# Another table of turns for a two-layer decoder: readers of norms, the router's choice and the tail's selection stand one or two turns later

## The reference

```
x = norm(x + splat_attention(x))          # 16 heads of 16, 256 keys, scores over 16 gaussians
x = norm(x + cross_attention(x, ctx))     # 16 heads of 16, 120 keys
x = norm(x + gate * expert[argmax](x))    # router over 8 experts, one 256x256 expert a token
x = norm(x + causal_attention(x))         # 16 heads of 16
y = norm_gain(x)                          # then two blocks, each:
y = y + block(y, y or ctx)                #   attention, 16 heads of 32, + li1, norm, li2 (1024), gelu, li3
x = norm(x + y)                           #   first block: 256 keys, kept only after the diagonal; second: ctx
x = norm(x + sum of 4 of 16 experts(x))   # sigmoid gates, top 4, hidden 64 an expert
```

## Time and profile before

| | |
|---|---|
| median of 3 runs | 3736.54 us (3733.85 to 3744.52) |
| the profiled execution | 3735.17 us |
| its span, first to last instruction | 3733.0 us |
| TensorE busy, matmuls | 3110.0 us, 83% |
| VectorE, ScalarE, GpSimd busy | 2682.5, 2104.6, 972.8 us |
| mean granted TensorE clock | 0.922 of full |
| idle of TensorE ahead of the transposes of `z` (L727) | 98.8 us on `z`, in 39 waits |
| on the key ring's DMA (L710) | 79.5 us, in 36 waits |

### The profile page before, as it was taken

The page is one execution under the profiler, slowest core; times in us unless marked ns, Lnnn a source line. Parts: engine busy times, 40 slices in busy tenths (PEclk is TensorE's granted clock), DMA queues, the critical chain, the costliest instruction groups (busy, mean ns, idle before and its releaser), DMA issues. The chain is left out here.

```text
span 3733.0 us, 89796 instructions
## 1 busy us (share of the span) xinstructions
PE 3110.0 (83%) x34864; PEld 2446.6 (66%) x34864; DVE 2682.5 (72%) x6391; ACT 2104.6 (56%) x4254; POOL 972.8 (26%) x1788
## 2 busy tenths in 40 slices
PE   1978888888788888988988888898988897988886
PEld 1767666767676767766766666676766676766664
DVE  5768676767676767767777667686776777868765
ACT  4746665556556554664565555646665556466642
POOL 0312341122233321231233222212342122124310
PEclk9999899989899989989999989998998999989987
DMA  6211211112212121121121111212121112112110
GB/s 199 71 55 58 74 57 61 44 44 60 64 50 77 50 63 43 49 67 53 48 74 58 54 54 38 70 45 72 59 69 60 38 42 70 48 60 71 60 37 6
DMA packets 362009, 221.50 MB, mean 59 GB/s; under 512 B 102497, under 2 KB 333299, under 8 KB 361587
## 3 DMA queue, kind: packets, MB, share of 16 engines
q1 hardware_dynamic: 361586, 215.76, 19.1%
HBM read 122.23 MB, written 93.32 MB: 58 GB/s over the span
## 5 line engine op out<-in xcount | busy, mean ns | idle before, releaser
L1150 ACT ACTIVATE p<-bank,p_log 128x512 f32<-128x512 f32 (+2 forms) x1280 | 748.4, 585 | 1104.1 <-PE bank L839 989.4
L1711 POOL TENSOR_TENSOR prob<-p,prob 120x256 f16<-120x256 f32 (+2 forms) x512 | 450.4, 880 | 1644.7 <-ACT prob L1151 1644.3
L1151 ACT ACTIVATE prob<-bank,p_log 128x512 f16<-128x512 f32 (+2 forms) x1280 | 749.6, 586 | 0.0
L1416 DVE TENSOR_REDUCE negm<-bank 128x2 f16<-128x512 f32 (+1 forms) x1024 | 511.3, 541 | 91.1 <-PE bank L803 87.7
L1339 DVE TENSOR_TENSOR prob<-p,prob 128x512 f16<-128x512 f32 (+2 forms) x768 | 487.8, 644 | 91.6 <-ACT prob L1151 87.5
L710 PE MATMUL bank<-w_exp,ident_h 128*128 128x512 f16 x1280 | 419.8, 412 | 95.6 <-DMA k_ring<-k_heads 79.5
L818 PE MATMUL bank<-q_ring,k_ring 80*128 80x256 f16 (+4 forms) x2048 | 443.7, 283 | 41.1 <-ACT raw L1097 14.6
L839 PE MATMUL bank<-ident_h,negm 128*128 128x256 f16 (+2 forms) x2560 | 441.4, 260 | 0.0
L1720 POOL TENSOR_SCALAR_AFFINE_SELECT probm<-prob 128x128 f16<-128x128 f16 x1024 | 327.2, 358 | 299.0 <-DVE prob L1339 299.0
L803 PEld LDWEIGHTS bank<-k_ring,q_ring 80*128 80x128 f16 (+1 forms) x2560 | 236.6, 104 | 234.3 <-issue 52.6
L803 PE MATMUL bank<-k_ring,q_ring 80*128 80x256 f16 (+4 forms) x2560 | 361.7, 259 | 33.9 <-DVE negm L1416 22.6
(11 more groups left out here) (293 smaller groups left out, 6261.9 us busy)
## 6 DMA issues: line engine op xcount, KB each, us to landing
q_ring<-q_heads SPq DMA_DIRECT2D x768, 40.0 KB, 2.1
q_heads<-q_made SPq DMA_DIRECT2D x96, 256.0 KB, 2.3
k_heads<-k_made SPq DMA_DIRECT2D x96, 256.0 KB, 2.3
q_ring<-q_heads SPq DMA_DIRECT2D x512, 48.0 KB, 2.1
k_ring<-k_heads SPq DMA_DIRECT2D x512, 40.0 KB, 2.2
q_heads<-q_made SPq DMA_DIRECT2D x144, 128.0 KB, 1.8
k_heads<-k_made SPq DMA_DIRECT2D x144, 128.0 KB, 1.8
k_ring<-k_heads SPq DMA_DIRECT2D x256, 48.0 KB, 2.2
```

The source lines that it names most:

```text
L1150: act(p32[0:n, g % PBUF32, 0:cols], ps[0:n, 0:cols], ACT.Exp, bias=p_log[0:n, :], scale=a.scale)
L1151: act(prob[0:n, 0, g % PBUF, 0:cols], ps[0:n, 0:cols], ACT.Exp, bias=p_log[0:n, :], scale=a.scale).then_inc(a_done, one(a_done))
L1416: v.tensor_reduce(negm[:, h * NT:(h + 1) * NT], scores[:, :].rearrange("p (t n) -> p t n", t=NT)[:, :, 0:ATTNS[k].keys], AX.X, ALU.max, ne ...
L1711: g.tensor_tensor(prob[0:n, 1, m % PBUF, 0:cols], p32[0:n, m % PBUF32, 0:cols], prob[0:n, 0, m % PBUF, 0:cols], ALU.subtract).then_inc(pp_ ...
```

## The change

The table gets other numbers. Nothing else is changed: no instruction is added or taken out, and each engine keeps the order of its stages but for those that now pass parts of the attention or a stage of another chain. Three stages of `LATE_SOON` come earlier by one.

```diff
@@ -152,20 +152,20 @@
 EARLY = {
     0: (),
     1: (("oT", 9), ("out", 12), ("out2", 14)),
-    2: (("oT", 9), ("out", 11), ("out2", 12), ("xT_e", 15), ("router", 17), ("best", 21), ("experts", 22), ("experts2", 26), ("experts3", 30)),
+    2: (("oT", 9), ("out", 11), ("out2", 12), ("xT_e", 16), ("router", 18), ("best", 22), ("experts", 24), ("experts2", 27), ("experts3", 30)),
     3: (("oT", 9), ("out", 13), ("norm2", 14), ("norm4", 19)),
     4: (("oT", 9), ("out", 11), ("out2", 12), ("ctx", 16), ("ctx2", 17), ("xoT", 18), ("h0", 22), ("h1", 23), ("h2", 26), ("norm3", 28), ("norm4", 30)),
-    TAIL: (("oT", 9), ("out", 11), ("out2", 12), ("xoT", 16), ("h0", 18), ("h1", 21), ("h2", 25), ("h3", 26), ("xT", 29), ("sel", 31)),
+    TAIL: (("oT", 9), ("out", 11), ("out2", 12), ("xoT", 17), ("h0", 19), ("h1", 22), ("h2", 25), ("h3", 26), ("xT", 31), ("sel", 33)),
 }
 LATE = {
     0: (("xT", 2), ("q_raw", 4), ("q", 7), ("k_raw", 10), ("k", 15), ("v", 18)),
     1: (("xT", 2), ("q", 9), ("k", 10), ("v", 13)),
     2: (("xT", 1), ("q", 10), ("k", 13), ("v", 18)),
     3: (("xT", 4), ("q", 9), ("k", 14), ("v", 17)),
-    4: (("xT", 1), ("q", 10), ("k", 14), ("v", 16)),
-    TAIL: (("gates", 2), ("r0", 4), ("r1", 8), ("r2", 10), ("r3", 11)),
+    4: (("xT", 3), ("q", 10), ("k", 14), ("v", 16)),
+    TAIL: (("gates", 4), ("r0", 6), ("r1", 9), ("r2", 11), ("r3", 12)),
 }
-LATE_SOON = {1: (("xT", 18), ("q", 21), ("k", 23), ("v", 28)), 3: (("xT", 22), ("q", 24), ("k", 25), ("v", 28))}
+LATE_SOON = {1: (("xT", 18), ("q", 20), ("k", 22), ("v", 27)), 3: (("xT", 22), ("q", 24), ("k", 25), ("v", 28))}
 VECTOR_ONLY = ("out2", "experts3", "norm4", "h3", "r3", "ctx2")
 ENGINES = "tensor", "scalar", "vector", "gpsimd"
```

## The result

The changed kernel takes 3826.26 us (median of 4 runs, 3815.76 to 3827.52) beside 3740.41 us for the kernel before in the same job: ratio 1.0219, 95% interval [1.0202, 1.0236], 82 us slower by the ratio (the medians lie 86 us apart). The prediction was 3751, range 3705 to 3782. Its direction held, its size did not: the time lies outside the range.

A forecast was written before the change was run, and what follows sets the result against it. TensorE, busy 83% of the span, was taken as the bound, waiting only where a turn precedes its data. Terms -2 + 0 + 3 - 13 + 5 + 17 + 5 + 0 = +15 us on 3735.17 gave 3750, as median 3751; range 3705 to 3782.

The forecast's parts named there:

- The sum leaves this as it is: TensorE's clock: about 580 us at the lower level stay, since old waits shrink and new ones of 1 to 2 us come.
- The tail's block at 0, bounds -24 and +12: (TAIL, xT), sel, gates, r0 later: shorter waits offset by the later choice and split of `inT`; 0 us, bounds -24 and +12.
- Rival 1: Tail and (4, xT): the choice of four and the masks are never late; -15 us, 3721 us; chance 0.2.
- r1, r2, r3 at +3, bounds 0 and +8: Tail's r1 to r3 one turn later: some 0.5 us less cover for `hidT` between r1 and r2; +3 us.
- (2, xT_e), router, best at -13, bounds -17 and -8: Stages of k = 2, later past R: 14 waits on `x` shorten, -14, router +1, best 0; -13 us.
- experts, experts2 at +5, bounds 0 and +8: Stages of k = 2, later: half of W less ahead of (2, xT), which already waits on `x`; +5 us.
- (TAIL, xoT), h0 at +17 and h1 at +5: Tail, one turn later: ScalarE's features behind exponentials delay h0, +17 us; less cover ahead of h2, +5 us.
- (4, xT) at -2: Turn 1 to 3, past W: shorter waits on `z`, against losses where masked attention makes W wait; -2 us, bounds -8 and +6.
- LATE_SOON at 0: q, k, v one turn earlier: gain or loss taken up by the key ring's DMA wait; 0 us, bounds -5 and +5.
- the signs named: TensorE's waits: `x` to about 18 us, `z` about 75, `tailT` gone, `raw` and `oT` up 15 to 20, new `inT` wait.
- Rival 4: Tail: h0 waits 2 us in all 16 tails (+32), the choice of four loses 12; +42 us, 3778 us; chance 0.15.

## Why the prediction was wrong, step by step

The steps that failed are the price of 0 for the tail's late block, which cost 43 to 49 us, the -13 for the router's stages, which cost 11, and the +3 for r1, which cost 12 to 18 of the block's; and the sum had no term for TensorE's busy time.

- **"The sum leaves this as it is"** (the clock) failed: the time at the lower level rose by 36 us in the traces and by 59 as means, worth at most 18 or 30 us. These are the same microseconds as those of the stages below, not a cause beside them. Half of the span's 80.8 us is busy time, and what part of it the clock does not explain stays open.
- **The tail's block at 0, bounds -24 and +12**: 43 to 49 us. The order of events was right (ScalarE's four exponentials, then the choice, then the split of `inT`), and the new wait at q_raw was named. The sizes were off. The choice was put to end 0.5 us later than now and the split at 648.05, where TensorE needs it at 648.54; no working is given for the 0.5. Counted from the transposes' start, the choice ends at 8.01 us where I had 6.7, and was at 6.18 before. Of these 1.83 us, 1.34 are the later start of sel's exponential (4.25 us behind the transposes, 2.91 before) and 0.49 the first step of the choice, which takes 0.67 us beside GpSimd's pass in place of 0.18. R and E between `z` and sel are at the lower level, R 1.25 us (646.72 to 647.97) where it takes 0.65 at full clock (656.99 to 657.64, the fence with r1 on 8); but they were so before too (1.21 us from 643.35), so a sum from the old trace should have had it. And in the phase shown what follows the wait runs slower as well. Rival 1 decided "from the point where q_raw waits under 0.5 us"; it waits 1.92.
- **r1, r2, r3 at +3, bounds 0 and +8**: 17.6 us alone, 12 beside sel on 32. I counted what lies between r1 and r2 and not what lies ahead of r1: that turn 9 has oT, that the lower k goes first, and that r1's 6.3 us had been the cover of `o_tok`. The sentence on it is missing, not mis-sized.
- **(2, xT_e), router, best at -13, bounds -17 and -8**: +11. The gain at `x` came (10.6 us in the list); a stage with the same turn as the router was overlooked, as with r1.
- **experts, experts2 at +5, bounds 0 and +8**: +15, of which the cause that I gave, the wait on `x`, shows 2.3.
- **(TAIL, xoT), h0 at +17 and h1 at +5**: 14 together. Mechanism and place right: the wait at h0 was put at 0.8 to 1.2 us a phase above 0.5, and was 1.93 in the instance, but 16.2 us in all, and at L700 the wait for `raw` went from 16.9 to 3.1 us in exchange while that for `oT`'s high part rose from 1.2 to 10.0, neither of which the sum had.
- **(4, xT) at -2**: +1 with an interval of 5 us to either side, the right size, but by luck. I had `z` falling to 75 and it fell to 37.2, since I took W to be ready; W waits for the same engine.
- **LATE_SOON at 0**: right.

Of the signs named, a new wait on `inT` at L704, almost none on `tailT` at L704 (0.5), `x` near 18 (20.6) and `oT` up by some 16 us held; `z` near 75 and the rise of `raw` did not. Rival 4 was the nearest, dear new waits for 42 us; it put them at h0, and they came in the tail's late block.

No version beats the kernel before. The ones with later turns that are not told from it by the bound of 0.3% are the two with r1 left on 8, 1.0004 and 1.0011, and (4, xT) alone.

## What to carry to other kernels

Where each engine follows one written order, a stage is not only late or early itself: it is what covers the waits of the stages around it. For each moved stage list what shares its new turn, in order, and what stood ahead of it; the price can lie there (r1 in front of oT, 18 us in one number). A wait that shrinks on one engine's list is a gain only if the engine that it waited for has less ahead of it: look for the same microseconds under another name before they are counted.

## What the runs showed of the hardware

- Time at the lower clock has no one price. As means over all executions, filled waits on `z` took off 102 us of it and no time; filled waits at q_raw and gates took off 107, with 19 us of time. Among the 87 executions of the kernel before (mean clock 0.918 to 0.927, 3731 to 3752 us) a straight line through the pairs gives 0.2 us of time for each us at the lower level, not 0.5.
- A second wait, of up to 3.1 us, behind the one on `z` did not raise the idle time as a whole: with sel on 33 and on 32 it is the same within 3.1 us, but the spans differ by 25.5 us, and the time at 1.2 GHz by 79 us in the two traces, by 36 as means.
- A short VectorE instruction that starts just behind a GpSimd pass ended with that pass: 0.66 to 1.15 us in 13 of 16 cases in place of 0.18, for the same 128x32 values.
- Traces of kernels that take the same time differ by up to 18.6 us in TensorE's busy time and 9.4 in its idle time. The split of a small loss into the two, read from one pair of traces, is not safe.
